# Key and query biases carried in the last row of their weights, and layer-norm statistics run in turn with the quantisation chains

## The reference

```python
x = x + 0.5 * _L0_ffn_ref(_layernorm(x), w_gate, w_up, w_down)    # FP4-quantised inputs and weights, silu(gate) * up
x = x + _L0_attn_ref(_layernorm(x), Wq, bq, Wk, bk, Wv, bv, ...)  # linear attention, 16 heads of 64, then its own FFN
x = x + 0.5 * _L0_ffn_ref(_layernorm(x), ...)                     # the FP4 FFN again
x = x + 0.5 * _L1_ffn_ref(_layernorm(x), w1, b1, w2, b2)          # relu FFN of width 512
x = x + _L1_attn_ref(_layernorm(x), Wk, bk, Wv, bv, Wf, bf)       # causal softmax attention, 16 heads, then gelu and Wf
x = x + 0.5 * _L1_ffn_ref(_layernorm(x), ...)
```

```python
q = src @ Wq + bq;  k = src @ Wk + bk
Q = elu(q) + 1;     K = elu(k) + 1
KV = einsum('bshd,bshm->bhdm', K, v);  Z = 1 / (einsum('bshd,bhd->bsh', Q, K.sum(axis=1)) + EPS)
```

## Time and profile before

| | |
|---|---|
| median of 3 timed runs | 1056.63 us (1055.36 to 1059.58) |
| the profiled execution, its own time | 1051.78 us |
| its span, first to last instruction | 1050.0 us |
| PE busy | 908.3 us (87% of the span) |
| DVE busy | 708.3 us (67%) |
| ACT busy | 510.4 us (49%) |
| POOL busy | 258.1 us (25%) |
| mean granted TensorE clock | 0.959 |
| longest chain: PE, DVE, ACT, POOL, issue, DMA | 60%, 19%, 7%, 6%, 6%, 1% |

### The profile page before, as it was taken

One profiled execution on the slowest core, in us unless ns is written; L12 is line 12 of the kernel. 1 busy time (PEld: TensorE's weight loads), 2 busy tenths in 40 slices (PEclk: granted clock), 3 DMA queues, 4 the chain that ended last, 5 costly groups with the idle time before them and its releaser, 6 DMA issues.

```text
span 1050.0 us, 19992 instructions
## 1 busy us (share of the span) xinstructions
PE 908.3 (87%) x7353; PEld 451.5 (43%) x7353; DVE 708.3 (67%) x1675; ACT 510.4 (49%) x886; POOL 258.1 (25%) x405
## 2 busy tenths in 40 slices
PE   2688888778898877887899989999999999999997
PEld 1344445555676665433433433243332224332225
DVE  7899963467887767468775577766678867677204
ACT  1133332244444322443556555766656675666774
POOL 1455530023556655413240000212000000000000
PEclk9899998899999988797899999999999999999999
DMA  5210000000000022031003200000400000000000
GB/s 181 56 36 1 0 1 1 1 1 1 2 1 1 2 58 34 2 77 28 13 23 67 37 17 15 14 2 14 94 18 12 2 11 5 17 4 12 6 8 12
DMA packets 30935, 23.20 MB, mean 22 GB/s; under 512 B 9609, under 2 KB 27897, under 8 KB 30840
## 3 DMA queue, kind: packets, MB, share of 16 engines
q1 hardware_dynamic: 29928, 21.39, 8.6%
q10 hardware_dynamic: 912, 0.54, 0.2%
HBM read 17.32 MB, written 4.34 MB: 21 GB/s over the span
## 4 chain that ended last, share of the span: by engine, by line
PE 60%; DVE 19%; ACT 7%; POOL 6%; issue 6%; DMA 1%; SPq 0%; ACTq 0%; DVEq 0%; POOLq 0%
PE psum L1704 12%; PE psum L1721 11%; PE psum L1678 7%; PE psum L1643 5%; DVE arena L1312 4%; PE psum L1590 3%; ACT arena L981 3%; PE psum L1559 2%; POOL rs L711 2%; PE psum L1396 2%; PE psum L1601 2%; PE psum L1437 2%; PE psum L1735 2%; PE psum L1363 2%; PE psum L1624 2%
## 5 line engine op out<-in xcount | busy, mean ns | idle before, releaser
L1312 DVE TENSOR_REDUCE arena<-psum 128x2 f32<-128x1024 f32 (+2 forms) x320 | 336.3, 1064 | 139.8 <-PE psum L1643 85.0
L981 ACT ACTIVATE arena<-psum 128x1024 f32<-128x1024 f32 (+3 forms) x320 | 284.7, 898 | 152.6 <-PE psum L1678 81.8
L1704 PE MATMUL psum<-arena 128*32 128x512 f32 (+3 forms) x1280 | 153.7, 553 | 1.3 <-ACT arena L981 1.3
L711 POOL TENSOR_TENSOR rs<-ve,mhalf 128x1 f32<-128x1 f32 x128 | 71.1, 561 | 333.7 <-DVE ve L1106 333.4
L1721 PE MATMUL psum<-arena,ones 128*32 128x512 f32 (+3 forms) x1280 | 150.5, 542 | 0.9 <-DVE arena L1339 0.8
L1643 PE MATMUL psum<-arena 48*128 48x512 bf16 (+3 forms) x640 | 112.7, 354 | 26.9 <-DVE arena L1312 9.8
L1678 PE MATMUL psum<-arena 50*128 50x512 bf16 (+3 forms) x640 | 114.5, 358 | 12.3 <-DMA arena<-arena 6.1
L1678 PEld LDWEIGHTS psum<-arena 50*128 50x128 bf16 x640 | 31.0, 93 | 191.7 <-issue 115.9
L817 POOL TENSOR_TENSOR arena<-arena 128x512 f32<-128x512 f32 x15 | 19.1, 1272 | 228.1 <-DMA arena<-scr_sums 228.1
L950 ACT ACTIVATE rh<-psum,fb 128x128 f32<-128x128 f32 x128 | 36.6, 368 | 58.3 <-PE psum L1590 58.3
L1643 PEld LDWEIGHTS psum<-arena 48*128 48x128 bf16 x640 | 35.6, 94 | 54.6 <-DVE arena L1312 19.0
(11 more groups left out here) (187 smaller groups left out, 1484.5 us busy)
## 6 DMA issues: line engine op xcount, KB each, us to landing
arena<-scr_parts SPq DMA_DIRECT2D x96, 64.0 KB
arena<-scr_sums SPq DMA_DIRECT2D x60, 64.0 KB, 2.0
scr_parts<-arena SPq DMA_DIRECT2D x12, 256.0 KB, 2.6
arena<-arena SPq DMA_DIRECT2D x124, 2.0 KB, 1.8
X<-in_L_attn_src_dram SPq DMA_DIRECT2D x4, 256.0 KB, 4.8
out_dram<-X SPq DMA_DIRECT2D x16, 64.0 KB, 1.6
arena<-in_c_zsel_dram SPq DMA_DIRECT2D x1, 512.0 KB, 4.0
arena<-in_L_attn_Wk_dram SPq DMA_DIRECT2D x1, 512.0 KB
```

What stands on the lines that cost most here:

```text
L711: v.tensor_tensor(rs[:, u, t:t + 1], ve[:, u, t:t + 1], mhalf[:, :], ALU.pow).then_inc(s_rstd[u], 1)
L981: v.activation(pr[:, u % RING, pp, :, 0:CH - off], both(("scores", n))[0][:, :, off:CH], ACT.Exp).then_inc(s_p, 1)
L1312: v.tensor_reduce(MXP[:, j, 2 * pp:2 * pp + 2, m], both(("max", g, pp, j, m))[0][:, :, 0:hi - lo], AX_X, ALU.max).then_inc(s_mxd, 1)
L1704: last = mm(bank(O_BANK)[VD * h:VD * h + VD, off:CH], V[kb // TPC][:, kb % TPC, GH * (g % GPC) + h, :], pr[:, u % RING, h // 2, h % 2, 0:C ...
```

## The change

The biases bk and bq get one added (for the elu form) and are written as the last row of Wk and Wq. The last weight rows, spread over all partitions in W7k and W7q, are taken off the other 127 rows by POOL. n_turn transposes the tile with ones instead of XN1. The bias matmuls of k and q go. The statistics of x and of the updated X become chains that run in turn with the quantisation chains; x's are made one iteration earlier. xo gets a third buffer; INVERT_AT and NORM_AT of the first chunk of the causal stage grow by two.

```diff
-FIRST_ORDER = [("h_turn", 3), ("x_turn", 1), ("x_stats", 0), ("quotients0", 0), ("add_stats_n", 4), ("g", 7),
-                ("quotients1", 0), ("quotients2", 0), ("n_turn", 5), ("down", 3), ("gate_up", 1),
-                ("quotients3", 0), ("k_ready", 6), ("k", 5), ("n_norm", 4)]
+FIRST_ORDER = [("h_turn", 3), ("x_turn", 1), ("add_stats_n", 4), ("quotients0", 0), ("x_stats", -1), ("g", 7),
+                ("quotients1", 0), ("n_norm", 5), ("quotients2", 0), ("n_turn", 5), ("down", 3), ("gate_up", 1),
+                ("quotients3", 0), ("k_ready", 6), ("k", 5)]
-INVERT_AT, NORM_AT = 3, 5
+INVERT_AT, NORM_AT = {0: 5, 1: 3, 2: 3, 3: 3}, {0: 7, 1: 5, 2: 5, 3: 5}
-        xo = [cb([D]), cb([D])]
+        xo = [cb([D]) for _ in range(3)]
+        W7k, W7q = KVT.rearrange("p a b -> p (a b)"), Mw.rearrange("p a b -> p (a b)")
@@ SP
-            for t, name in ((Wk, "Wk"), (Wq, "Wq"), (W1, "W1")):
-                sp.dma_start(t, A["L0_attn_" + name]).then_inc(s_ld["b"], 16)
+            for k, (t, w7, name) in enumerate(((Wk, W7k, "Wk"), (Wq, W7q, "Wq"))):
+                sp.dma_start(t[0:D - 1, :], A["L0_attn_" + name][0:D - 1, :]).then_inc(s_ld7[k], 16)
+                sp.dma_start(w7, A["L0_attn_" + name][D - 1, :].partition_broadcast(P)).then_inc(s_ld7[k], 16)
+            sp.dma_start(W1, A["L0_attn_W1"]).then_inc(s_ld["b"], 16)
...
+            sp.wait_ge(s_elu, 1)
+            sp.dma_start(sce, welu).then_inc(s_elud, 16)
+            sp.wait_ge(s_elud, 16)
+            for k, t in enumerate((Wk, Wq)):
+                sp.dma_start(t[D - 1:D, :].rearrange("o (a n) -> o a n", n=P),
+                             sce[HD // P * k:HD // P * (k + 1), :].unsqueeze(0)).then_inc(s_ldkq[k], 16)
             sp.wait_ge(s_rows, 1)
@@ POOL
+                if nx == KEY_ROWS_AT:          # 3
+                    less_last_row(0, Wk, W7k)
+            def less_last_row(k, w, w7):
+                pool.wait_ge(s_ld7[k], 32)
+                v.tensor_tensor(w[0:D - 1, :], w[0:D - 1, :], w7[0:D - 1, :], ALU.subtract).then_inc(s_wkq, 1)
             def value_weights(t):
+                if t == 6:
+                    less_last_row(1, Wq, W7q)
@@ ACT, n_ones
-                if t >= 2:
-                    act.wait_ge(s_g, t - 1)
-                v.copy(xo[t % 2][:, 0:D - 1], XN1[:, t, 0:D - 1]).then_inc(s_xo, 1)
+                if t >= 3:
+                    act.wait_ge(s_g, t - 2)
+                v.copy(xo[t % 3][:, 0:D - 1], XN1[:, t, 0:D - 1]).then_inc(s_xo, 1)
@@ DVE
             def x_stats(n):
+                if n < TILES:
+                    chains.append(first_stats(n))
+                    if n == 0:
+                        in_turn_for(chains, 100)
+                    return
...
             def add_stats_n(t):
-                add_down(t)
-                in_turn(stats(1, t, X[:, t, :]))
+                chains.append(down_stats(1, t))
@@ PE
             def n_turn(t):
-                pe.wait_ge(s_n1, t + 1)
+                pe.wait_ge(s_xo, t + 1)
-                nc.tensor.transpose(bank(6)[:, P:2 * P], XN1[:, t, :], ident[:, :]).then_inc(s_n1t, 1)
+                nc.tensor.transpose(bank(6)[:, P:2 * P], xo[t % 3], ident[:, :]).then_inc(s_n1t, 1)
             def k(t):
                 if t == 0:
-                    pe.wait_ge(s_ld["b"], 16 * 12)
-                    pe.wait_ge(s_bias, 16 * 3)
-                    pe.wait_ge(s_set, 6)
+                    pe.wait_ge(s_wkq, 1)
+                    pe.wait_ge(s_ldkq[0], 16)
...
-                    bias(bank(2 + n), BIAS_K + 512 * n, 512)
                     last = mm(bank(2 + n), XNT[:, P * t:P * t + P], Wk[:, 512 * n:512 * n + 512],
-                              start=False, stop=True, skip_group_check=True)
+                              start=True, stop=True)
@@ PE, queries
-                    mm(o, bias_rows[:, BIAS_Q + P * j:BIAS_Q + P * j + P], onesb[:, 0:GRP], start=True,
-                       stop=False, skip_group_check=True)
```

More of the change, by code:

```diff
@@ L70 @@
 QUOTIENT_PARTS = 4
+KEY_ROWS_AT = 3
+X_FROM = 1
 TILES_BEHIND = 6
@@ L374, in at_iteration @@
             for name, lag, *which in order:
-                if name.startswith("quotients"):
+                if name.startswith("quotients") and k >= 0:
                     out.append(("quotients", int(name[-1]), k + run, k + run - 2, count + run))
-                elif 0 <= k - lag < count:
+                elif not name.startswith("quotients") and 0 <= k - lag < count:
                     out.append((name, k + run - lag))
@@ L381, in first_pass @@
         def first_pass():
-            return [x for i in range(TILES + 7) for x in at_iteration(FIRST_ORDER, i, TILES, 0)]
+            return [x for i in range(-1, TILES + 7) for x in at_iteration(FIRST_ORDER, i, TILES, 0)]
         def second_pass():
@@ L469, in causal @@
                 if g + 1 < MGROUPS:
[L470 to L473, removed]
+                    put(end + INVERT_AT[c], "invert", g)
+                    put(end + INVERT_AT[c], "store_inverse", g)
+                    put(end + INVERT_AT[c] + 1, "spread_inverse", g)
+                    put(end + NORM_AT[c], "norm", g)
                 if g % GPC == GPC - 1:
@@ L1037, in _ @@
             v.memset(eps[:, :], 0.0).then_inc(s_set, 1)
-            for n in range(2):
+            for n in range(3):
                 v.memset(xo[n][:, D - 1:D], 1.0).then_inc(s_set, 1)
@@ L1084, in split_bias @@
                 rows = slice(0, BIAS_END // P)
-                elu = wrow[0:2 * HD // P, :]
                 dve.wait_ge(s_ld["row"], 16 * 7)
-                me.wait(me.did(v.tensor_scalar(elu, elu, 1.0, None, ALU.add)))
+                v.tensor_scalar(welu, welu, 1.0, None, ALU.add).then_inc(s_elu, 1)
                 me.wait(me.did(v.tensor_copy(wrowb[rows, 0, :], wrow[rows, :])))
@@ L1111, in normed, with first_stats @@
                 return v.tensor_scalar(y, x, mv[:, u, t, 0:1], rs[:, u, t:t + 1], ALU.subtract, ALU.mult)
-            def x_stats(n):
-                if n < TILES and n % 4 == 0:
-                    dve.wait_ge(s_ldx[n // 4], 16)
-                if n >= TILES:
-                    dve.wait_ge(s_xb, tile(n) // 2 + 1)
+            chains = []
+            def first_stats(n):
+                if n % 4 == 0:
+                    dve.wait_ge(s_ldx[n // 4], 16)
+                yield from stats(0, n, X[:, n, :])
+            def x_stats(n):
+                if n < TILES:
[3 more added lines that the diff above has]
+                    return
+                dve.wait_ge(s_xb, tile(n) // 2 + 1)
                 in_turn(stats(0, tile(n), X[:, tile(n), :]))
@@ L1143, in h_to_fp4 @@
                 yield from quantise(hb[:, :], hv[:, s, :], hm[:, s, :], hs[:, s], GI // BLK, s_hr)
-            chains = []
             def quotients(part, nx, nh, end):
@@ L1150, in quotients @@
                         chains.append(h_to_fp4(nh))
+                if part == (X_FROM if nx < TILES else 0):
                     if nx < end:
@@ L1169, in add_down, with down_stats @@
                                        in1=X[:, t, :], op0=ALU.mult, op1=ALU.add).then_inc(s_xa, 1)
+                yield
                 dve.wait_ge(s_xa, n + 1)
+            def down_stats(u, n):
+                yield from add_down(n)
+                yield from stats(u, tile(n), X[:, tile(n), :])
             def add_stats_n(t):
-                add_down(t)
-                in_turn(stats(1, t, X[:, t, :]))
+                chains.append(down_stats(1, t))
             def n_norm(t):
@@ L1276, in add_stats_d @@
             def add_stats_d(n):
-                add_down(n)
-                in_turn(stats(4, tile(n), X[:, tile(n), :]))
+                in_turn(down_stats(4, n))
             def f_stats(n):
```

30 lines of the change are left out of this document (21 added, 9 removed).

## The result

| | before | changed kernel |
|---|---|---|
| median, us | 1055.99 (1053.45 to 1059.58, 4 runs) | 1083.23 (1081.46 to 1089.76, 4 runs) |
| profiled execution: its time, span, granted clock | 1051.78, 1050.0, 0.959 | 1084.83, 1082.9, 0.943 |

The ratio is 1.0275, with a 95% interval of 1.0239 to 1.0312: slower, 3 us from the forecast of 1080. The medians and ratios of the experiments leave out runs over 1.5% above the fastest of their kernel: two of ten in e2, one of nine in e5, five of twelve in e11 (with them the medians are 1047.47, 1047.51 and 1048.06).

What follows compares the result with a forecast made beforehand. DVE's stream was taken to pace the first pass, PE close behind; neither alone bounds the second. +39.3 - 10.1 - 3.0 + 1.2 - 1.0 - 2.5 = +23.9 on 1051.78 gives 1075.7, plus 4.85 for the median: 1080.5, rounded to 1080; range 1064 to 1093.

Steps and rivals of the forecast that it cites:

- Loads: Weight loads on SP: three 127-row loads share one DMA engine, adding 40.6 us; first k of tile 0 39.3 us later.
- The period: First pass, time per tile from k of tile 0 on: falls from about 7.6 to 6.8 us, bounds 6.5 and 7.6.
- the port of xn: First pass: xn's new place beside POOL's work on h may cost what n_norm's new place gives on DVE.
- a rival of 7.0 us: First pass: by the shared-port rule the period would be 7.0 us instead of 6.8; no chance given.
- The subtraction for Wq stalls DVE like the one for Wv, 1.32 - 0.16 = +1.2: First pass: POOL's last-row subtraction for Wq stalls a DVE tensor_scalar, costing +1.2 us.
- The first interval: First pass, first k to the next: set by k, exp, k_ready and a slow-clocked PE, 5.9 us instead of 7.6.
- Ten tiles: First pass, ten tiles from k of tile 0: 67.1 us instead of 77.2, a gain of 10.1.
- the last five: End of first pass, last five tiles: 29.7 us before, shorter by 3.0.
- The terms for queries: 64 bias matmuls go: -1.0 us in the middle stage, -2.5 in the second pass (bounds 0 and -6.2).
- The inversion's 0: Causal stage: the later inversion is worth 0, since PE waits longer for another DMA; the later norm costs nothing.

Runs made afterwards that it cites:

- e2: Changed kernel with the 127-row loads of Wk and Wq each cut into 112 and 15 rows, Wv's left whole: 1045.95 us, ratio 0.9934.
- e5: e3 with the first causal chunk's INVERT_AT and NORM_AT back at 3 and 5: 1044.88 us, ratio to before 0.9900.
- e11: e3 with each of POOL's three last-row subtractions cut into four of 256 columns: 1042.15 us, ratio to before 0.9902.
- e1: Kernel before with only Wk and Wq loaded as 127 rows plus one row: 1094.39 us, ratio 1.0369.
- e7: Changed kernel with the DRAM round trip of bk + 1 and bq + 1 issued ahead of the weights' loads on SP: 1057.74 us, ratio to before 1.0021.
- e12: Changed kernel with Wq's 127-row load issued by ACT instead of SP: 1084.62 us, ratio to before 1.0303.
- e4: e2 with the statistics, n_norm and start of x's chain back where the kernel before has them: 1057.35 us, ratio to before 1.0022.
- e10: e6 with the statistics, n_norm and start of x's chain back where the kernel before has them: 1053.04 us, ratio to before 0.9996.
- e9: e6 with the first causal chunk's INVERT_AT and NORM_AT back at 3 and 5: 1037.32 us, ratio to before 0.9867.
- e6: e3 with POOL's subtractions for Wv and Wq moved from tiles 4 and 6 to 12 and 14: 1036.39 us, ratio to before 0.9806.
- e8: Kernel before with only Wv's 127-row load cut into 112 and 15 rows: 1053.22 us, ratio 0.9974.
- e3: e2 with Wv's 127-row load also cut into 112 and 15 rows: 1049.56 us, ratio to before 0.9929.

## Why the prediction came out

**Loads, right.** One engine for all three, +40.6 us on it: the store moved by 41.0, the first k by 38.4 to 38.6 where 39.3 was forecast. e1, e2, e7 and e12 show each link: the form of the load, the engine, the hold on SP, and the DMA that stands behind.

**The period, right in size, with one premise off.** 6.8 us was forecast and 6.86 measured. The prediction took DVE's stream for what sets the pace in the kernel before. The chain that ended last says so only up to 98 us (7.57 us from one k_ready to the next in the earlier trace rows); from there to tile 10 and beyond it runs through PE and ACT, 7.65 us a tile: k, g, ACT's copies (they stand behind n_ones, which waits for g with two buffers), n_turn, down, gate_up, k again. From the chain of before, and of the changed kernel (start us, us, what):
```profile
124.17 1.73 PE psum L1447 x4
...
126.18 0.37 ACT hqT L862
...
127.02 0.30 PE psum L1425
127.31 0.73 PE psum L1417 x6
```
```profile
109.10 0.43 DVE hv L1081
...
110.42 0.52 DVE hv L1091
110.94 1.13 DVE arena L1223
```
So before there were two loops of nearly one length. In e4 and e10, with the third buffer and without the bias matmuls, the chain runs through DVE at 7.57; with the statistics moved as well, at 6.86. That the statistics and n_norm take 0.7 us off DVE's loop is shown. That they would do so with PE's loop left at 7.65 is not: that kernel was not run, and the 15.7 us of e10 against e9 are what they bring on top of the biases and the third buffer. For the port of xn the prediction used the Trainium skill, "SBUF — State Buffer", "SBUF: two separate sides", for a rival of 7.0 us; the stall it describes is there (0.75 against 0.34, and 2.48 against 0.34 beside the subtraction), but the sum of the chains left more than it took.

**The step that failed is "The subtraction for Wq stalls DVE like the one for Wv, 1.32 - 0.16 = +1.2".** It took the length of a stall from the earlier trace rows, where a tensor_scalar of 128x8 met the subtraction near its end. How long a stall is depends on where in POOL's 2.35 us DVE's next tensor_scalar falls. In the new order the 128x352 one falls at its very start, 2.14 us each, and for both weights, Wv's included, whose subtraction I had left at its old price. After each, PE has waited 2.9 to 3.3 us and k takes 3.65 us instead of 1.9 (granted clock 0.89 over the 16 us around it), and the next interval is 7.67: 0.8 more. That makes (2.15 + 0.8) x 2 = 5.9 where 1.2 stands. e6 shows it: at 6.9 us of first pass. The 0.8 does not always come: in e5 PE waited as long after the first subtraction, its k kept its 1.96 us, and the next interval was 6.85; in e7 it was the same. What decides whether the clock falls there is open.
```profile
94.16 1.96 PE L1475 MATMUL psum<-arena 128*128 128x512 f32 x4 [2.87 <-DVE arena L1225]
101.01 1.96 PE L1475 MATMUL psum<-arena 128*128 128x512 f32 x4 [0.72 <-DVE arena L1225]
```

**The first interval, wrong by 1.8.** I had k, exp and k_ready in it, 5.9 us (the terms written there, 1.7 + 1.1 + 1.2 + 1.7, make 5.7). It was 7.72: in PE's order h_turn, x_turn, n_turn, down and gate_up stand between two k, n_turn waits 1.55 us for ACT, and the second took 7.17. Ten tiles came to 75.97 us against 67.1 + 1.2 forecast and 77.17 before; the last five to 25.8 for a forecast of 26.7.

**Biases.** The terms for queries were -1.0 in the middle stage and -2.5 in the second pass. The middle stage came out 4.0 shorter, the second pass (first to eighth out_add) 0.7. Neither is a measurement of the bias matmuls: the same instructions of the middle stage took 31.9 to 36.4 us in the changed kernel and its variants. What differs between these two profiles is the granted clock at its start. mix_kv's 16 matmuls, before and after:
```profile
171.24 3.52 PE L1464 MATMUL psum<-arena 128*128 128x128 f32 x16
```
```profile
202.56 1.95 PE L1500 MATMUL psum<-arena 128*128 128x128 f32 x16
```
Windows of 12 us there show a granted clock of 0.82 before (160 to 172) and 1.00 after (198 to 210). By e10 (0.9996, 0.9961 to 1.0031) the biases alone bring nothing that can be told from 4 us to either side.

**Causal stage.** The inversion's 0 holds as far as e5 and e9 can tell. But the profile of after is 9.0 us longer here, which I did not forecast, and which does not look like the change's: e8, with the causal stage of the kernel before to the letter, took 536.3 us and waited 10.06 for the maxima; e2, with that of the changed kernel, 531.4 and 5.97. Over 14 profiles the four kernels beside before that have the old place of the inversion lie at 532.4 to 537.9 and the eight others beside the changed kernel at 528.9 to 537.1. The profile before (529.8) is near the short end of them and the one after (538.8) beyond the long one. So a stage that differed by chance is the likeliest home of the 6 us by which the profiles differ more than the medians; only one profile of each kernel was taken. What sets the landing of those DMAs in one execution was not tried.

**Net.** Forecast +23.9 on the profile, measured +33.1 there and +27.2 in the medians. Of the errors, 7.7 in ten tiles, 1.8 in the second pass and 9 of a long causal stage add; 3.0 of the middle stage, 0.9 each of the first k, the last five tiles and the end, and 3.65 of the stretch between the second pass and the causal stage, go the other way; that last stretch took 75.0 to 80.3 us in the changed kernel and its variants, so it may be chance as well. Errors of 18.5 us one way met 9.4 the other, and the medians moved 6 less than the profiles. The time landed close because the term that decides was right; that it landed within 3 us is luck.

## What to carry to other kernels

Look at the row count of a load before its bytes: one engine moved 127 rows of 4 KB in 20 us, and held every later issue of its queue; in 112 and 15 rows, two statements each, Wk and Wq brought the first k back from 90.47 to 52.78. A big GpSimd instruction is priced by the VectorE instruction that meets it, so after reordering VectorE the place of each must be looked at again, and the repair that worked here was a place where VectorE waits anyway. And a stage far from the edit that has changed by several microseconds should be looked up in a second kernel with the same stage before it is explained.

## What the hardware showed that I had not expected

- A load of 127 rows issued on ACT's queue lengthened the hold of SP's queue from 9.12 to 26.66 us: the two queues share the engine, and SP, which issued next, was held for both loads.
- In pieces, POOL's subtraction took 3.21 us for 2.35, and DVE's tensor_tensors beside it 0.81 and 1.04 for 0.28 and 0.52: both engines were slower at once, where with one long instruction only DVE was. A part of POOL's 0.86 us is the cutting itself: Wk's four pieces took 2.79, with DVE idle for the first 0.75 us of them.
- Runs of one kernel on one chip spread by up to 15 us, 1.5% (e7: 1050.54 to 1065.06, e10: 1045.9 to 1061.23). In e7 the time goes with the mean granted clock (0.953 to 0.961 in its four shortest runs, 0.947 to 0.952 in its six longest), in e10 it does not (0.961 in the shortest, 0.960 in the longest). One run of each kernel would not have told e2, e3, e5 or e11 apart from before.
